# Masked attention in a fused decoder block: a quarter of the attention weights turned by VectorE and transfers instead of TensorE

## The reference, cut to what matters

```python
Q = query @ Wq.T + bq;  K = key @ Wk.T + bk;  V = value @ Wv.T + bv      # split into heads
energy = jnp.einsum('bhqd,bhkd->bhqk', Q, K) / np.sqrt(HEAD_DIM)
energy = jnp.where(mask == 0, jnp.float32(-1e+20), energy)
attention = jax.nn.softmax(energy, axis=-1)
x = jnp.einsum('bhqk,bhkd->bhqd', attention, V)
return x.transpose(0, 2, 1, 3).reshape(b, -1, D_MODEL) @ Wo.T + bo
```

## Time and profile before

| what | value |
|---|---|
| median of 3 runs | 1990.67 us (1990.65 to 1991.74) |
| profiled execution | 1987.96 us |
| its span, first to last instruction | 1986.2 us |
| TensorE matmul busy | 1941.3 us (98%) |
| VectorE, ScalarE, POOL busy | 1232.3, 1112.4, 600.2 us |
| granted TensorE clock | 0.998 of full speed |
| attention slots | 975.7 to 1247.4 us of the span |

### The profile page before, as it was taken

One profiled execution on the slowest core, in us unless ns is written; L12 is line 12 of the kernel. 1 busy time (PEld: TensorE's weight loads), 2 busy tenths in 40 slices (PEclk: granted clock), 3 DMA queues, 4 the chain that ended last, 5 costly groups with the idle time before them and its releaser, 6 DMA issues.

```text
span 1986.2 us, 43991 instructions
## 1 busy us (share of the span) xinstructions
PE 1941.3 (98%) x17307; PEld 1694.8 (85%) x17307; DVE 1232.3 (62%) x3579; ACT 1112.4 (56%) x2432; POOL 600.2 (30%) x652
## 2 busy tenths in 40 slices
PE   6999999999999998998999999999999999999998
PEld 6898998989898984777688887889999999999998
DVE  7767777776767666776688988438758623243212
ACT  5666666666666663333577877544444444444443
POOL 3111141112211101233122211444444444444444
PEclk9999999999999999999999999999999999999999
DMA  5656454455445431000311011001010010101000
GB/s 202 185 174 205 148 166 151 151 174 151 158 152 166 144 123 48 1 1 1 92 43 37 25 33 40 6 1 64 1 43 22 22 43 1 43 1 43 1 12 32
DMA packets 100332, 154.21 MB, mean 78 GB/s; under 512 B 12896, under 2 KB 78752, under 8 KB 100000
## 3 DMA queue, kind: packets, MB, share of 16 engines
q1 hardware_dynamic: 100128, 151.41, 24.3%
HBM read 103.73 MB, written 43.45 MB: 74 GB/s over the span
## 4 chain that ended last, share of the span: by engine, by line
PE 46%; ACT 2%; DVE 2%; issue 1%; POOL 0%; POOLq 0%; DVEq 0%; ACTq 0%
PE bank L83 21%; PE bank L1132 18%; PE bank L1053 2%; PE bank L1068 1%; PE bank L1040 1%; ACT att_p L1238 1%; PE bank L1098 1%; PE bank L1009 1%; ACT att_pt L1243 1%; PE bank L1079 0%; DVE dec_room L140 0%; POOL right_h L963 0%; ACT att_kt L1230 0%; PE bank L1091 0%; DVE att_vz L1385 0%
## 5 line engine op out<-in xcount | busy, mean ns | idle before, releaser
L963 POOL TENSOR_TENSOR right_h<-right_hr,right_h 128x512 fp32r<-128x512 f32 x256 | 340.9, 1332 | 418.3 <-ACT right_hr L1285 418.3
L1284 ACT ACTIVATE right_h<-bank,dec_b 128x512 fp32r<-128x512 f32 x256 | 176.3, 689 | 389.6 <-PE bank L83 365.0
L83 PE MATMUL bank<-lat_kv_t,lat_qk 128*128 128x320 f32 x1536 | 253.7, 314 | 2.8 <-DVE lat_qk L2456 2.8
L83 PE MATMUL bank<-lat_wv,lat_kv_t 128*128 128x512 f32 x960 | 242.1, 393 | 0.0
L83 PEld LDWEIGHTS bank<-lat_kv_t,lat_qk 128*128 128x128 f32 x1536 | 227.6, 188 | 15.5 <-DVE lat_qk L2456 6.4
L2320 ACT ACTIVATE lat_p<-bank,lat_neg_max 128x320 f32<-128x320 f32 x256 | 134.6, 527 | 148.4 <-DVE lat_neg_max L2461 148.4
L83 PEld LDWEIGHTS bank<-lat_wv,lat_kv_t 128*128 128x128 f32 x960 | 175.1, 188 | 30.4 <-DVE lat_qk L2456 0.4
L83 PE MATMUL bank<-dec_xt,dec_lo 128*128 128x512 f32 x512 | 200.7, 392 | 0.0
L2461 DVE TENSOR_REDUCE lat_neg_max<-bank 128x1 f32<-128x320 f32 x256 | 122.5, 486 | 93.6 <-PE bank L83 87.6
L1285 ACT ACTIVATE right_hr<-bank,dec_b 128x512 f32<-128x512 f32 x256 | 174.4, 681 | 0.0
L1132 PE MATMUL bank<-dec_hi,right_h 128*128 128x256 f32 x1024 | 161.6, 280 | 1.2 <-POOL right_h L963 1.2
(11 more groups left out here) (332 smaller groups left out, 3806.6 us busy)
## 6 DMA issues: line engine op xcount, KB each, us to landing
lat_turns<-lat_pb SPq DMA_DIRECT2D x63, 640.0 KB, 3.0
lat_pt<-lat_turns SPq DMA_DIRECT2D x252, 160.0 KB, 3.2
raw_w<-in_L_ffn_W SPq DMA_DIRECT2D x16, 1024.0 KB, 6.6
lat_ctx_raw<-in_ctx SPq DMA_DIRECT2D x16, 512.0 KB, 5.3
right_ctx_raw<-in_ctx_turned SPq DMA_DIRECT2D x16, 512.0 KB, 3.7
lat_kv_f<-in_ctx_turned SPq DMA_DIRECT2D x15, 512.0 KB, 4.3
lat_ctx_raw<-gate_rows SPq DMA_DIRECT2D x15, 512.0 KB, 4.8
lat_kv_t<-lat_lt SPq DMA_DIRECT2D x32, 128.0 KB, 4.4
```

Source lines behind the costliest of these rows:

```text
L83: mm = pe.matmul(out, lhs(a, k), rhs(b, k), start=first and k == 0 and n == 0, stop=last and k == KD - 1 and n == 2)
L963: pool.tensor_tensor(h[:, g % 2, 1, :], hr[:, g % 2, :], h[:, g % 2, 0, :].bitcast(F32), ALU.subtract).then_inc(h_lo, 1)
L1284: act.activation(h[:, n % 2, 0, :], h_bank[n % 2][:, :], ACT.Relu, bias=bias).then_inc(h_hi, 1)
```

## The change

The weights m=0, r=0 and 1 (a quarter) are no longer transposed by TensorE. VectorE transposes them in 32x32 blocks into `pb`; SP writes `pb` to device memory and reads it back in four pieces, so that the blocks land where the full transpose needs them (`pt_early`). TensorE turns r=2, 3 of m=0 (`turn_mid`) and the four of m=1 (`turn_late`). `weigh` runs both halves in one, behind all copies, the transfers and the values. ScalarE copies the late turned weights after two exponentials instead of one, and takes over the high copy of the context, later in the slot. The values' bias is no longer added to the values: since the weights of a row sum to one, its product with Wo is added once to bo (`output_bias`). `vz` has three places instead of two; the values' copies stay with VectorE and come before `slot_early`. The exponentials of m=0 are written over their scores.

```diff
+            def weights_out(b):
+                sp.wait_ge(p_turned, b + 1)
+                wait(sp, pt_in[b % 2], 64 * (b // 2))
+                sp.dma_start(turns[b % 2], pb[:, :, :, :].rearrange("p g u c -> p (g u c)")).then_inc(p_out, 16)
+            def weights_back(b):
+                sp.wait_ge(p_out, 16 * (b + 1))
+                wait(sp, o_psum, b)
+                for g in range(4):
+                    sp.dma_start(pt_early[g * 32:(g + 1) * 32].rearrange("p q r t c -> p q (r t c)"),
+                                 turns[b % 2].rearrange("(q p) (g c) -> g p q c", q=4, g=4)[g]).then_inc(pt_in[b % 2], 16)
             load_weights(0)
-            for i in range(2, NT):
-                context(i)
+            context(2)
+            for b in range(B):
+                weights_out(b)
+                weights_back(b)
+                if b % 2 == 1 and (b + 5) // 2 < NT:
+                    context((b + 5) // 2)
...
+            def turn_mid(b):
+                pe.wait_ge(p_ready, 8 * b + 4)
+                wait(pe, pt_done, 3 * b - 1)
+                turn_half(b, 0, 1)
+            def turn_late(b):
+                pe.wait_ge(p_ready, 8 * b + 6)
+                pe.wait_ge(pt_done, 3 * b + 1)
+                turn_half(b, 1, 0)
+                pe.wait_ge(p_ready, 8 * b + 8)
+                if b in in_slot:
+                    pe.wait_ge(*read_out(*in_slot[b]))
+                turn_half(b, 1, 1)
+            def weigh(b):
+                pe.wait_ge(pt_done, 3 * b + 3)
+                pe.wait_ge(pt_in[b % 2], 64 * (b // 2 + 1))
+                pe.wait_ge(v_done, b + 1)
...
             for b in range(B):
                 energies(b)
+                if b == 0:
+                    output_bias()
                 if b >= 1:
-                    turn(b - 1, 1)
+                    turn_late(b - 1)
                 if b + 1 < B:
                     keys_proj(b + 1)
                 if b >= 1:
-                    weigh(b - 1, 0)
-                    weigh(b - 1, 1)
-                turn(b, 0)
+                    weigh(b - 1)
                 if b + 1 < B:
                     values_proj(b + 1)
+                turn_mid(b)
...
@@ ScalarE
                 weights_of(b, 0, 0)
+                weights_of(b, 0, 1)
                 if b >= 1:
-                    turn(b - 1, 1)
-                for r in range(1, R):
-                    weights_of(b, 0, r)
+                    turn_late(b - 1, 0)
+                    turn_late(b - 1, 1)
                 if b + 1 < B:
                     keys_proj(b + 1)
-                turn(b, 0)
-                for r in range(R):
-                    weights_of(b, 1, r)
+                weights_of(b, 0, 2)
+                weights_of(b, 0, 3)
+                if b % 2 == 0 and b // 2 + 1 < NT:
+                    split_keys(b // 2 + 1)
+                weights_of(b, 1, 0)
+                weights_of(b, 1, 1)
+                weights_of(b, 1, 2)
+                turn_mid(b)
+                weights_of(b, 1, 3)
...
@@ VectorE
             def values_proj(b):
                 dve.wait_ge(v_psum, b + 1)
...
-                    ins = dve.tensor_tensor(to[:, :, at:at + HD], src[:, :, par, :], bias[:, :, par, :], ALU.add)
+                    ins = dve.tensor_copy(to[:, :, at:at + HD], src[:, :, par, :])
                 ins.then_inc(v_done, 1)
+            def turn(b):
+                dve.wait_ge(p_ready, 8 * b + 2)
+                wait(dve, p_out, 16 * b)
+                dve.transpose(pb[:, :], p[0][:, 0:2].rearrange("p r (t g c) -> p g (r t) c", g=4, c=32)).then_inc(p_turned, 1)
...
-                lowest(b, 0, 0, R)
+                lowest(b, 0, 0, 2)
+                lowest(b, 0, 2, R)
+                turn(b)
                 lowest(b, 1, 0, R)
-                if b % 2 == 0 and b // 2 + 1 < NT:
-                    split_keys(b // 2 + 1)
+                if b == 0:
+                    output_bias()
                 if b % 2 == 1:
                     add_bias(b // 2)
                 if b >= 1:
                     normalise(b - 1)
-                slot_early(b)
                 if b + 1 < B:
                     values_proj(b + 1)
+                slot_early(b)
                 slot_late(b)
```

More of the change, by code:

```diff
@@ L890, in _ @@
                 sp.dma_start(mask_i[half * S:(half + 1) * S, :], w["mask_1x1xSxS2_ik1"]).then_inc(loads, 16)
-            for t in range(2):
-                sp.dma_start(bv[:, t, :], everywhere(w["L1_xattn_bv"])).then_inc(loads, 16)
+            with nc.allow_non_contiguous_dma(reason="a bias as a column"):
+                sp.dma_start(bv[:, :], column(w["L1_xattn_bv"])).then_inc(loads, 16)
             sp.dma_start(bo[:, :], everywhere(w["L1_xattn_bo"])).then_inc(loads, 16)
@@ L938, in _ @@
             sp.wait_ge(b2_in, 16)
[L939 removed]
+            sp.wait_ge(loads, 80)
             sp.wait_ge(late_loads, 16 * 20)
@@ L1042, in energies @@
                 mm.then_inc(s_psum, 1)
-            def turn(b, m):
-                for half in range(2):
-                    pe.wait_ge(p_ready, 8 * b + 4 * m + 2 * half + 2)
-                    if 2 * b + m >= 1:
-                        pe.wait_ge(pt_done, 2 * (2 * b + m) - 1 + half)
-                    if m == 1 and half == 1 and b in in_slot:
-                        pe.wait_ge(*read_out(*in_slot[b]))
-                    for n in range(2):
-                        for t in range(2):
-                            mm = pe.transpose(pt_bank[half][:, (2 * n + t) * P:(2 * n + t + 1) * P],
-                                              p[:, m, 2 * half + n, t * P:(t + 1) * P], k.ident[:, :])
-                    mm.then_inc(pt_psum, 1)
@@ L1057, in weigh, with turn_half @@
[L1057 to L1072 removed]
+            def turn_half(b, m, half):
+                bank = pt_bank[0 if m == 0 else half]
+                for n in range(2):
+                    for t in range(2):
+                        mm = pe.transpose(bank[:, (2 * n + t) * P:(2 * n + t + 1) * P],
+                                          p[m][:, 2 * half + n, t * P:(t + 1) * P], k.ident[:, :])
+                mm.then_inc(pt_psum, 1)
@@ new lines, in turn_mid, with output_bias @@
+            def turn_mid(b):
[10 more added lines that the diff above has]
+                turn_half(b, 1, 1)
+            def output_bias():
+                pe.wait_ge(bv_cols, 1)
+                for m in range(KD):
+                    mm = pe.matmul(projected(0), ot[:, 0, m, :], wo[:, m, :], start=m == 0, stop=m == KD - 1)
+                mm.then_inc(bv_psum, 1)
@@ L1191, in _ @@
             hidden(0, 0)
-            turn(B - 1, 1)
-            weigh(B - 1, 0)
-            weigh(B - 1, 1)
+            turn_late(B - 1)
+            weigh(B - 1)
             for n in range(1, E * STEPS):
@@ L1236, in weights_of, with turn_mid, turn_late, split_keys @@
                 if m == 1 and r == 0 and b >= 1:
-                    act.wait_ge(pt_psum, 4 * b)
-                act.activation(p[:, m, r, :], sc[:, m, r, :], ACT.Exp, bias=low[:, m, r:r + 1], scale=-1.0).then_inc(p_ready, 1)
-            def turn(b, m):
-                for half in range(2):
-                    act.wait_ge(pt_psum, 2 * (2 * b + m) + half + 1)
-                    act.copy(pt[:, m, 2 * half:2 * half + 2].rearrange("p r t n -> p (r t n)"),
-                             pt_bank[half][:, :]).then_inc(pt_done, 1)
+                    act.wait_ge(pt_psum, 3 * b)
+                if m == 0 and r == 0:
+                    wait(act, p_turned, b)
+                if m == 0 and r == 2:
+                    wait(act, pt_psum, 3 * b - 2)
+                act.activation(p[m][:, r, :], sc[:, m, r, :], ACT.Exp, bias=low[:, m, r:r + 1], scale=-1.0).then_inc(p_ready, 1)
+            def turn_mid(b):
+                act.wait_ge(pt_psum, 3 * b + 1)
+                act.copy(pt_mid[:, :].rearrange("p r t n -> p (r t n)"), pt_bank[0][:, :]).then_inc(pt_done, 1)
+            def turn_late(b, half):
+                act.wait_ge(pt_psum, 3 * b + 2 + half)
+                act.copy(pt_late[:, 2 * half:2 * half + 2].rearrange("p r t n -> p (r t n)"), pt_bank[half][:, :]).then_inc(pt_done, 1)
+            def split_keys(i):
+                if i >= 2:
+                    act.wait_ge(ctx_in[i % 2], 16 * (i // 2))
+                    act.wait_ge(v_psum, 2 * i - 2)
+                act.copy(ctx_t[:, i % 2, 0], ctx_raw[:, i % 2]).then_inc(c_hi, 1)
             def side_read(kind, c, j):
@@ L1330, in _ @@
                     side_read(*in_slot[b])
-            turn(B - 1, 1)
+            for half in range(2):
+                turn_late(B - 1, half)
             for n in range(E * STEPS):
```

81 lines of the change are left out of this document (45 added, 36 removed).

## The result

The changed kernel is slower. It took 1993.71 us (median of 20 runs, 1992.59 to 1996.31) against 1989.45 for the kernel before (20 runs, 1988.11 to 1991.74): ratio 1.0023, 95% interval 1.0017 to 1.0028. That is a small loss, 0.2%, but it is outside the noise. Forecast were 1985.7 us and a gain of 5.0. The forecast started from the 1990.67 us of the first three runs, 1.2 more than the median of 20. The profiled execution took 1993.88 us for a span of 1992.1, 5.9 more than before. The 32 slots take 263.1 us from the first energies to the last (258.2 before); the first slot starts 0.65 later, and what follows slot 31's start is 0.35 longer.

A forecast was written before the change was run, and what follows sets the result against it. TensorE's sequence was taken as the bound. Gains of 3.15 (slots 1 to 9), 2.0 (10 to 15), 2.0 and 0.35 (later slots), less 1.7, 0.3 and 0.5, made 5.0 us: 1990.7 to 1985.7, range 1980 to 1993.5.

The forecast's parts named there:

- around the slots: Outside the attention slots: the spread bias column and the tail were to cost 0.5 us.
- TensorE's bound: Attention slots: TensorE's work after VectorE's first `lowest` sets the length, saving 0.35 us per undisturbed slot, not 0.51.
- D: Moment VectorE begins a slot's first `lowest`, 1.22 us after an undisturbed slot's start; weighing was forecast at D+2.39.
- plain slots: Attention slots without side work: forecast 6.65 us odd and 7.5 even, from 7.0 and 7.87.
- Rival A: Attention stage: TensorE stays the bound, 3 to 8 us gained, 1985.7 us; chance 0.5.
- the price of what POOL's subtraction falls beside: Late part of even slots: `cell_apply` meeting the second subtraction in slots 10, 18 and 26 priced at 0.5 us each.
- the row: Profile row of `normalise` beside POOL's subtraction: 0.77 us against 0.29, so 0.48 lost, used to price the new neighbours.
- the 1.90 of `expert0_low`: VectorE in slot 20, before `moe_apply`: D of slot 21 1.7 late instead of 1.1, losing 0.5; slot 29 repeats it.
- B: Attention stage: VectorE takes the whole gain, 4 of the 5 us go, 1989.7 us; chance 0.25.
- C: Turned weights' round trip through device memory decides: at 7.5 us against 6.88 allowed, 3 us slower, 1993.5; chance 0.17.
- the queue's order: SP's queue: only the next context load stands behind the transfers, needed three slots later; round trip 6.0 us, hidden.
- The bias product: Slot 0: the added biases' product (0.43), with ScalarE's order setting the end, was to cost 0.3 us.

The follow-up runs named there:

- side_first: Changed kernel with the biases' product ahead of the loop and ScalarE's context copies at the end of even slots, behind its side work; 1979.88 us, ratio 0.9954.
- pe_turn: Changed kernel with the first quarter of the weights turned by TensorE again, no block transpose and no transfers; 2009.55 us, ratio 1.0104.
- nosub_after: Changed kernel with POOL's subtraction cut to 8 columns from context 2 on; 1982.51 us, ratio to the kernel before 0.9968.
- copy_back: Changed kernel with the high copy of the context back on VectorE after its lowest scores; 1990.55 us, ratio to the kernel before 1.001.
- early_ctx_bias: Changed kernel with ScalarE's context copies at the end of even slots, ahead of its side work, and the biases' product ahead of the loop; 1986.2 us, ratio 0.9986.
- move_alone: Kernel before with only the high context copies moved to ScalarE, behind its side work at the end of even slots; 1985.09 us, ratio 0.9979.

## Why the prediction was wrong

The slot table of the prediction against the two profiles, in us (plus is longer), with `side_first` beside it:

```
                        predicted   after - before   side_first - before
slot 0                    +0.3          +2.41            -0.02
slots 1 to 9              -3.15         -1.64            -1.83
slots 10 to 15            -2.0          -1.07            -2.67
slots 16, 17, 21, 29      +1.7          +4.69            -0.79
slots 18, 22, 23, 26, 30  -2.0          -1.92            -1.93
slots 20, 28              -0.35         -0.43            +0.06
slots 19, 24, 25, 27       0            +2.87            -2.07
around the slots          +0.5          +1.00            +2.24
sum                       -5.0          +5.91            -7.01
```

**TensorE's bound held.** Weighing at D+2.39 was D+2.38; plain slots of 6.65 and 7.51 were 6.70 and 7.56; a late slot saves only by its D. The block transpose was 0.71 as on the line between the earlier trace rows, `normalise` 0.29, ScalarE's copy 1.04 for 1.05. Slots 18 to 30 that were priced at 0.4 each gained 1.92 for 2.0. `pe_turn` against the changed kernel shows from the other side that the turn gains. Rival A's mechanism is right for the plain slots, and the gain of the turn is real; it was spent elsewhere.

**The step that failed is the price of what POOL's subtraction falls beside.** The prediction saw that the moved copy moves the subtraction, and priced the new neighbours at 0.5 in each of slots 10, 18 and 26, by `normalise`'s 0.48, and at nothing in all others. The price was wrong because the row was read as a fixed loss for a wait. In slot 6 of the kernel before, the first of POOL's two instructions of the earlier trace rows ends at 1023.96; `normalise`, which starts 0.66 after POOL's start, ends at 1024.11, 0.15 after POOL's end.

```profile
1022.68 1.28 POOL L953 TENSOR_TENSOR right_ctx_t<-right_ctx_raw,right_ctx_t 128x512 fp32r<-128x512 f32 x1 [12.28 <-DVE right_ctx_t L1355]
```

In the profile before, 15 of 15 such multiplications that start while a POOL instruction runs end 0.15 us after it; in the changed kernel, so do 14 of 14 operations of `cell_apply` and `moe_apply`. The 0.48 came of what was left of POOL's instruction (0.62 us) when `normalise` met it, and of nothing else. An operation that starts just behind POOL's loses nearly the whole of it: `cell_apply` of slot 10 lost 1.05, the scan 0.96 (0.69 to 1.65) and the operation ahead of it 0.20, the four `moe_apply` 0.96 (1.37 to 2.33, all of it in the first) and `expert0_low` 0.45. The places were wrong too: `moe_apply` and the scans stand at the end of slots 16, 20, 24 and 28, and the late D that comes of it goes to the slots after. D of slots 11, 17, 19, 21, 25, 27 and 29 was 1.0 to 1.4 us later than without the subtraction. Without the subtraction the changed kernel is 11.2 us faster, more than twice the loss (in the profiles 3.1 of 11.6 are clock falls), and `side_first` shows that it is the place and not the amount of POOL's work.

The Trainium skill (SBUF — State Buffer, SBUF: two separate sides) had it: the port pair is an exclusive lock, taken by VectorE for an operation with two SBUF inputs or in a two-port mode. The traces agree: VectorE's end follows POOL's by 0.15, and the other way round, a POOL subtraction of slot 20 that met `expert0_low` took 2.25 instead of 1.27. The trace doesn't show whether `cell_apply`, with one input, ran in a two-port mode. Traces here agree also in what is spared: `lowest`, which reads a PSUM bank and the mask, stays at 420 ns beside the subtraction, and the block transpose at 712. The prediction weighed that rule and took the row instead. Taken literally, the rule gave 1.3 for each of the three slots, nearer to the 1.05 measured; but even by the rule the prediction counted three slots. A second slip of the same kind: the 1.90 of `expert0_low`, from which the loss in slots 21 and 29 was reckoned, stood beside the subtraction itself; alone it takes 1.18. With the subtraction out of the way, in `side_first`, slots 16, 17, 21 and 29 together gained 0.79 where 1.7 were to be lost.

**The clock was not in the prediction.** The granted clock fell to 0.50 (1.2 GHz) for 3.4 us twice inside the stage of the changed kernel, in slots 0 and 29, never in that of before. In slot 29 the stretches before, in and after read:

```profile
1217.35:1220.00 2.65, 2.65 (x31) 2.30 (x31) 2.65 (x5) 1.27 (x3) 1.83 (x1) 1.00 0.09 25
1220.00:1223.40 3.40, 1.43 (x41) 1.22 (x43) 3.40 (x19) 2.38 (x6) 0.00 (x0) 1.00 0.00 0
1223.40:1226.90 3.50, 3.50 (x60) 3.33 (x48) 2.33 (x10) 2.21 (x6) 0.00 (x0) 0.51 0.35 118
1226.90:1229.47 2.57, 2.57 (x24) 1.70 (x22) 2.22 (x4) 0.99 (x2) 0.00 (x0) 1.00 0.18 50
```

TensorE had waited 1.97 us for ScalarE's late copy just before. In slot 0 the wait was 1.47, and the keys' twelve products then took 3.08 us instead of 1.68. A fall cost 1.5: slot 29 12.12 against 10.62, slot 0 8.19 against 6.64. So a late D can be paid for twice, and the two falls make 3.0 of the 5.9 us between the profiles. The one in slot 0 isn't shown to come from the change: the kernel before has the same wait of 1.47 without a fall, and `nosub_after` and `copy_back` have the same slot 0 in 6.64. Only one execution of each kernel was profiled, so how often the falls occur is not known. Of the rivals B had the right engine, but no loss beyond the gain (1989.7); C had the right number (1993.5) by a mechanism that didn't take place.

**Slots 1, 3 and 5** gave nothing, where 1.05 was forecast, and each for a reason of its own. In slot 1 TensorE waits 0.29 for ScalarE's copy of the turned weights, behind the context's copy in slot 0; `copy_back`, with that copy on VectorE, has 6.70 there. Slot 3 is 0.36 late by the subtraction once more: two preparing operations of VectorE at the end of slot 2 stand beside it, one of 128x16 elements for 1.18 us instead of 0.17, and `nosub_after` has 6.69.

```profile
997.59 2.56 POOL L975 TENSOR_TENSOR right_ctx_t<-right_ctx_raw,right_ctx_t 128x512 fp32r<-128x512 f32 x2 [11.07 <-ACT right_ctx_t L1302]
999.00 1.18 DVE L1667 TENSOR_TENSOR dec_wrs<-dec_wr,dec_wrs 128x16 fp32r<-128x16 f32 x1
```

Slot 5 did wait for the transfers. Its weighing came at D+2.72: the transfer out was issued at 1009.33 behind the 512 KB load of the next context and the way back 3.76 later, where most batches have 2.0 to 2.7. The last piece landed at 1017.37, and the weighing started at 1017.46.

```profile
1008.02 0.43 SPq L891 DMA_DIRECT2D right_ctx_raw<-in_ctx_turned  x1
1009.33 0.34 SPq L930 DMA_DIRECT2D att_turns<-att_pb  x1
1013.09 1.74 SPq L936 DMA_DIRECT2D att_pt_early<-att_turns  x4
1016.89 0.34 SPq L930 DMA_DIRECT2D att_turns<-att_pb  x1
1019.03 1.25 SPq L936 DMA_DIRECT2D att_pt_early<-att_turns  x3
```

The prediction put only the queue's order beside that load, not its 3.9 us of landing. Batches 8, 9 and 10 have 3.8, 3.4 and 4.1 from out to back and were in time all the same. So in the changed kernel the transfers cost 0.35 in one slot, and rival C's 8 us are excluded. In other versions they met other slots: slot 7 of `nosub_after` (7.17 instead of 6.69) and slot 8 of `early_ctx_bias` (8.87 instead of 7.57). What makes the way long there isn't settled.

**The bias product** made slot 0 0.86 longer (6.64 in `nosub_after`, without a fall), not 0.3: TensorE does its four products and the order behind it waits for ScalarE's keys. Moved ahead of the loop it gains 1.0 us in both pairs of medians. The ranges of single runs overlap in both, and the start of the first slot varies more than that between the versions with it ahead (975.6 to 979.0), so its size stays uncertain.

## What to carry to other kernels

When a copy moves from one engine to another, list what it releases, and lay the released operation over the new neighbours one by one; here a subtraction on GpSimd cost 2.6 us in one place, 11.2 in a second (with the clock falls that went with it) and hardly anything in a third. The neighbours that it left alone here were VectorE's minimum with one input in PSUM, its copies from PSUM and its block transposes, and the place is best chosen so that the release comes just ahead of them. Look also at what stands behind the released operation in its own engine's order, since it moves too. Don't take a loss from a mean: compare the end of the held instruction with the end of the one that holds it. The price is what is left of the holder's instruction, and it counts where the slot's end is VectorE's.

## What the runs showed of the hardware that was not expected

- Some VectorE operations that start while a GpSimd instruction runs lasted until 0.15 us after that instruction's end: 15 of 15 two-input 128x128 multiplications from SBUF in the kernel before (0.29 alone, up to 0.88 in slots 2 to 28), 14 of 14 one-input 128x256 operations from SBUF in the changed kernel (0.41 alone, up to 1.36 beside a 128x512 subtraction, 0.82 beside a 128x256 addition). A scan went from 0.69 to 1.65, a three-operand 128x256 from 0.43 to 1.28, a 128x16 from 0.17 to 1.18. The masked minimum from PSUM (0.42), the copies from PSUM (0.42) and the block transposes from SBUF (0.71) kept their times.
- Eleven falls of the granted clock to 0.50 were met in slots 0 to 30 of six kernels, and ahead of each TensorE had stood idle for 1.46 to 2.30 us; that wait had ended up to 1.6 us before the fall. A twelfth, in slot 31 of `nosub_after`, had only waits of 1.04 and 0.68 ahead of it. The reverse doesn't hold: the version with TensorE's turn and early copies has waits of up to 2.3 and no fall. A fall costs some 1.5 us when it meets a full TensorE, and 0.8 in slot 0 of `move_alone` (6.56 against 5.77); what decides between a fall and none is open.
